# Masked attention: the values' products and the second chunk's turned rows issued behind the first scores, the fifth tile's rows normalised inside the first step

## What is computed

```python
def _L1_xattn_ref(q, k, v, mask, Wq, bq, Wk, bk, Wv, bv, Wo, bo):
    Q = _split_heads(q @ Wq.T + bq)
    K = _split_heads(k @ Wk.T + bk)
    V = _split_heads(v @ Wv.T + bv)
    scores = jnp.einsum('bhqd,bhkd->bhqk', Q, K) / math.sqrt(DV)
    scores = jnp.where(mask, jnp.asarray(1e-09, scores.dtype), scores)
    attn = jax.nn.softmax(scores, axis=-1)
    ctx = jnp.einsum('bhqk,bhkd->bhqd', attn, V)
    ...
    return ctx @ Wo.T + bo
x = x + _L1_xattn_ref(_layernorm(x, axis=-1), ctx_1024, ctx_1024, mask_1x1xSxS2_bk0, ...)
```

## Time and profile before

| what | value |
|---|---|
| median of 3 runs | 1599.02 us (1591.99 to 1600.58) |
| the profiled execution, its own time | 1598.18 us |
| its span, first to last instruction | 1596.4 us |
| what lies around the span | 1.78 us |
| mean granted clock of PE | 0.973 of full speed |
| busy in the span: PE, DVE, ACT, POOL | 1481.8, 1183.3, 881.6, 493.4 us |

### The profile page before, as it was taken

One profiled execution on the slowest core, in us unless ns is written; L12 is line 12 of the kernel. 1 busy time (PEld: TensorE's weight loads), 2 busy tenths in 40 slices (PEclk: granted clock), 3 DMA queues, 4 the chain that ended last, 5 costly groups with the idle time before them and its releaser, 6 DMA issues. The chain is left out here.

```text
span 1596.4 us, 30696 instructions
## 1 busy us (share of the span) xinstructions
PE 1481.8 (93%) x10998; PEld 1088.1 (68%) x11022; DVE 1183.3 (74%) x2306; ACT 881.6 (55%) x2091; POOL 493.4 (31%) x436
## 2 busy tenths in 40 slices
PE   6789999999999999789998997999999977998997
PEld 4567777777777777534443456888888866776785
DVE  4467887786777765368887966888888856788876
ACT  1334443334444344456557836888888874664332
POOL 0122222222222221200001534545555433665333
PEclk9799999999999999989999998999999998999999
DMA  6501111110111101113303810000000006215641
GB/s 243 202 7 50 43 43 53 65 42 8 36 34 34 42 12 76 43 73 145 135 12 122 359 52 2 3 2 3 3 3 4 3 1 263 81 75 169 206 159 58
DMA packets 47280, 118.35 MB, mean 74 GB/s; under 512 B 9406, under 2 KB 15934, under 8 KB 45504
## 3 DMA queue, kind: packets, MB, share of 16 engines
q1 hardware_dynamic: 41488, 100.03, 17.5%
q0 software_dynamic: 5680, 16.85, 2.7%
HBM read 78.89 MB, written 39.80 MB: 74 GB/s over the span
## 5 line engine op out<-in xcount | busy, mean ns | idle before, releaser
L1684 ACT ACTIVATE c_probs<-c_score,c_minus_top 128x128 f32<-128x128 f32 x512 | 183.7, 423 | 1.5 <-DVE c_minus_top L1781 1.5
L1642 POOL TENSOR_TENSOR c_probs<-c_probs,c_recip 128x1024 f32<-128x1024 f32 x64 | 121.5, 1899 | 175.7 <-DVE c_recip L1787 175.7
L629 POOL TENSOR_TENSOR a_attn_lo_parts<-a_attn,a_attn_hi_parts 128x512 fp32r<-128x512 f32 x64 | 80.3, 1288 | 250.0 <-ACT a_attn_hi_parts L695 250.0
L1684 ACT ACTIVATION_READ_ACCUMULATOR c_probs<-c_score,c_minus_top 128x1 f32 x512 | 134.2, 262 | 0.0
L691 ACT COPY a_attn<-a_pv_ps 128x512 f32<-128x512 f32 x64 | 37.0, 578 | 162.6 <-PE a_pv_ps L965 162.6
L928 PE MATMUL a_bank<-a_x_hi_parts,a_wq_hi 128*128 128x256 f32 x512 | 107.8, 293 | 4.3 <-POOL a_x_lo_parts L625 4.3
L928 PE MATMUL a_bank<-a_x_lo_parts,a_wq_hi 128*128 128x256 f32 x512 | 104.3, 286 | 0.0
L655 ACT ACTIVATE a_q<-a_bank,a_shift,a_gain 128x256 f32<-128x256 f32 x64 | 32.3, 556 | 130.2 <-PE a_bank L919 130.2
L928 PE MATMUL a_bank<-a_x_hi_parts,a_wq_lo 128*128 128x256 f32 x512 | 104.1, 285 | 0.0
L2204 ACT CAST d_xT_hi<-d_turn 128x512 fp32r<-128x512 f32 x71 | 41.7, 587 | 110.9 <-PE d_turn L2448 103.9
L911 PE MATMUL a_bank<-a_wo_hi,a_attn_hi_parts 128*128 128x512 f32 x256 | 102.3, 400 | 0.0
(11 more groups left out here) (302 smaller groups left out, 4337.4 us busy)
## 6 DMA issues: line engine op xcount, KB each, us to landing
hidden<-b_hidden SPq DMA_DIRECT2D x5, 2816.0 KB, 8.1
b_hidden<-hidden SPq DMA_DIRECT2D x5, 2816.0 KB, 11.4
xres<-in_x SPq DMA_DIRECT2D x8, 1024.0 KB, 14.1
d_we<-in_we SPq DMA_DIRECT2D x8, 1024.0 KB, 13.0
xres<-in_w_gate_up SPq DMA_DIRECT2D x7, 1024.0 KB, 5.2
d_got<-rows SPq DMA_DIRECT2D x20, 258.0 KB, 2.9
xres<-rows SPq DMA_DIRECT2D x19, 258.0 KB, 2.8
a_rot<-in_rot SPq DMA_DIRECT2D x16, 256.0 KB, 3.1
```

Of the source, the lines that this page charges most:

```text
L629: nc.gpsimd.tensor_tensor(of_spread(attn_lo, g), of_spread(attn, g), of_spread(attn_hi, g), ALU.subtract).then_inc(attn_lo_ready, 1)
L1642: nc.gpsimd.tensor_tensor(part, part, recip[:, t % 2, heads].unsqueeze(2).to_broadcast([P, HALF, KEYS]), ALU.mult).then_inc(scaled, 1)
L1684: last = nc.scalar.activation(probs[:, t, at, :], score_ps[:, h, g, :], ACT.Exp, bias=minus_top[:, h, g:g + 1], accum_out=total[:, t, at:a ...
```

## The change

Three things are put in another place; none is added or removed.

1. On PE the queries of chunk 0 and the scores of tile 0 come directly behind the turned rows of tiles 0 and 1. Behind the scores stand the turned rows of tiles 2 and 3, and behind those the values.
2. On DVE `c_x_lo_parts` of tiles 2 and 3 goes into the first step, behind both `find_tops` of tile 0. The normalising of tile 4 goes behind the first `invert`, with the two additions that write `c_vals` in its middle. `c_wo_lo` goes to the end of the first step.
3. On POOL `deviation` and `add_bias` of tile 4 go behind the first `scale` of tile 0.

The waits follow: PE waits for the values only at the first `weigh`. The diff, cut to its core:

```diff
-        PRE = ["act"] * KB + ["act"] * KB + ["dve"] * NT + ["dve"] * B + ["act"] * KB + ["dve"] * NT
-        PRE_K, PRE_T, PRE_V = KB, 2 * KB, 2 * KB + NT
-        PRE_Q, PRE_T2 = PRE_V + B, PRE_V + B + KB
+        PRE = ["act"] * KB + ["act"] * KB + ["dve"] * NT + ["act"] * KB + ["dve"] * NT + ["dve"] * B
+        PRE_K, PRE_T, PRE_Q = KB, 2 * KB, 2 * KB + NT
+        PRE_T2, PRE_V = PRE_Q + KB, PRE_Q + KB + NT
...
-                deviation(2 * NT, 0)
-                add_bias(2 * NT)
...
                             scale(tile, t, 0)
+                        if isinstance(n, int) and tile == 0:
+                            deviation(2 * NT, 0)
+                            add_bias(2 * NT)
...
-                for b in range(B):
-                    dve.wait_ge(bank_full, PRE_V + b + 1)
-                    nc.vector.tensor_tensor(vals[:, b], bank[(PRE_V + b) % NB][:].rearrange("p (h d) -> p h d", d=DH1),
-                                            bv[:].rearrange("p (h d) -> p h d", d=DH1), ALU.add).then_inc(freed["dve"], 1)
-                dve.wait_ge(weight_hi, 2)
-                nc.vector.tensor_tensor(wo_lo[:], wo[:], wo_hi[:], ALU.subtract).then_inc(weight_lo, 1)
-                for tile in range(NT):
-                    x_low(NT + tile, 1, tile, bank[(PRE_T2 + tile) % NB])
-                norm_stats(2 * NT, 0)
-                norm_row(2 * NT, 0)
-                head = ch.k
+                head, FIRST_STEPS = ch.k, 2
+
+                def beside_first(part):
+
+                    if part == 0:
+                        for tile in range(NT):
+                            x_low(NT + tile, 1, tile, bank[(PRE_T2 + tile) % NB])
+                        return
+                    norm_stats(2 * NT, 0)
+                    for b in range(B):
+                        dve.wait_ge(bank_full, PRE_V + b + 1)
+                        nc.vector.tensor_tensor(vals[:, b], bank[(PRE_V + b) % NB][:].rearrange("p (h d) -> p h d", d=DH1),
+                                                bv[:].rearrange("p (h d) -> p h d", d=DH1), ALU.add).then_inc(freed["dve"], 1)
+                    norm_row(2 * NT, 0)
...
                             find_tops(tile, j, t, 1)
+                        if first:
+                            beside_first(0)
...
                             invert(tile, t, 0)
+                        if first:
+                            beside_first(1)
...
                             x_low(tile + 2 * NT, j, t, use(n, j, t, "T").out)
+                        if first:
+                            dve.wait_ge(weight_hi, 2)
+                            nc.vector.tensor_tensor(wo_lo[:], wo[:], wo_hi[:], ALU.subtract).then_inc(weight_lo, 1)
...
                 for t in range(NT):
                     turn_x(t, t, pre_begin(PRE_T + t))
+                pe.wait_ge(weight_lo, 1)
+                pe.wait_ge(freed["dve"], ring.count("dve", PRE_Q))
+                for m in range(KB):
+                    project(pre_begin(PRE_Q + m), 0, m)
+                pe.wait_ge(freed["act"], PRE.count("act"))
+                scores(0, 0, 0, 0)
+                for t in range(NT):
+                    turn_x(NT + t, t, pre_begin(PRE_T2 + t))
                 pe.wait_ge(ld_wv, 16)
                 for b in range(B):
...
-                pe.wait_ge(weight_lo, 1)
-                pe.wait_ge(freed["dve"], ring.count("dve", PRE_V))
-                for m in range(KB):
-                    project(pre_begin(PRE_Q + m), 0, m)
-                for t in range(NT):
-                    turn_x(NT + t, t, pre_begin(PRE_T2 + t))
-
-                pe.wait_ge(freed["act"], PRE.count("act"))
-                scores(0, 0, 0, 0)
...
-                                pe.wait_ge(freed["dve"], PRE.count("dve"))
+                                pe.wait_ge(freed["dve"], ring.count("dve", PRE_V))
...
+                            if isinstance(tile, int) and tile == 1:
+                                pe.wait_ge(freed["dve"], PRE.count("dve"))
```

More of the change, by code:

```diff
@@ L1818, in _ @@
                     norm_row(tile, tile % 2)
-                for b in range(B):
-                    dve.wait_ge(bank_full, PRE_V + b + 1)
-                    nc.vector.tensor_tensor(vals[:, b], bank[(PRE_V + b) % NB][:].rearrange("p (h d) -> p h d", d=DH1),
-                                            bv[:].rearrange("p (h d) -> p h d", d=DH1), ALU.add).then_inc(freed["dve"], 1)
-                dve.wait_ge(weight_hi, 2)
-                nc.vector.tensor_tensor(wo_lo[:], wo[:], wo_hi[:], ALU.subtract).then_inc(weight_lo, 1)
-                for tile in range(NT):
-                    x_low(NT + tile, 1, tile, bank[(PRE_T2 + tile) % NB])
-                norm_stats(2 * NT, 0)
-                norm_row(2 * NT, 0)
-                head = ch.k
+                head, FIRST_STEPS = ch.k, 2
[10 more added lines that the diff above has]
+                    norm_row(2 * NT, 0)
                 def body(n, j, b, b_before, b_next):
                     if left(n, 2):
-                        ch.base, ch.k = n * DVE_STEPS + head, 0
+                        ch.base, ch.k = n * DVE_STEPS + (head + FIRST_STEPS), 0
+                    if isinstance(n, int) and n == 0:
+                        ch.base = head
                     for t, s in enumerate(plan(n)):
                         tile = n * NT + t
+                        first = isinstance(n, int) and tile == 0
                         if t < NT:
@@ L1856, in body @@
                             x_low(tile + 2 * NT, j, t, use(n, j, t, "T").out)
-                    assert not left(n, 3) or ch.k == DVE_STEPS, ch.k
+                        if first:
+                            dve.wait_ge(weight_hi, 2)
+                            nc.vector.tensor_tensor(wo_lo[:], wo[:], wo_hi[:], ALU.subtract).then_inc(weight_lo, 1)
+                    assert not left(n, 3) or ch.k == DVE_STEPS + (FIRST_STEPS if isinstance(n, int) and n == 0 else 0), ch.k
                 all_chunks(dve, body)
```

## The result

The changed kernel takes 1601.58 us (median of 20 runs, 1598.27 to 1603.38); over the same number of runs the kernel before takes 1595.9 us (1591.99 to 1600.58). The ratio is 1.0031, 95% interval [1.0023, 1.0039]: 4.9 us slower by 1595.9 x 0.0031, between 3.7 and 6.2; the two medians themselves lie 5.7 us apart. The profiled execution of the changed kernel took 1598.27 us, as long as that of before (1598.18). So positions are given from here on as distances from that matmul, **M**. The stage, from M to the first instruction of the expert stage on POOL, took 386.5 us before (1327.71 - 941.21) and 390.3 us now (1327.70 - 937.42).

A forecast was written before the change was run, and what follows sets the result against it. PE was taken to bound the masked stage, with the place that matters its pipeline fill, 6.28 us idle ahead of PT0. Terms 1.95 + 0.5 + 0.1, say 2.6 us, took 1598.18 to 1600.8; range 1594.6 to 1606.1.

The forecast's parts named there:

- third rival: PE's clock falls already in the new gaps of 1.5 and 0.6 us, delaying the exponentials 2.9 us: 1603.7; chance 0.1.
- the fifth: Rival: the start's shift is lost in later stages, the expert stage starting at another clock phase: 1597.9 to 1603.7; chance 0.09.
- forecast 2.45: On PE, PT0 and all behind it come 2.45 us later: idle time ends 1.95 later, plus 0.5 for turning tile 4.
- Step 10: Rest of step one: `c_wo_lo` makes POOL's second scaling end about 2.2 us late, costing PE 0.1 us at PT2.
- second rival: At the second scaling DVE waits for POOL, so tile 1's maxima come 1.2 us past 986.2: 1602.0; chance 0.12.
- due place: The exponentials of tile 1 on ACT were due at 986.2, which is 983.76 + 2.45.
- cover of 0.4 us: Tile 1's maxima stand at 985.8, its exponentials are due at 986.2; without this cover each further DVE microsecond costs one.
- step 9: PE's clock falls in the idle time ahead of PT0 and returns 5.9 us after restart, as before: no extra cost.
- The bound of 2.9 us either way: Bounds on PE's clock cost: no low stretch, or a second of the same length; half of 5.9 us.
- The drain behind a table load: Rival: a drain follows ACT's table load, so the exponentials start 1.4 us later: 1602.2; chance 0.03.

The follow-up runs named there:

- e2: Changed kernel with ACT's query of Qa put behind the exponentials of tile 0, in the first step alone; ratio to before 0.9991.
- b1: Kernel before, with ACT's query of Qa put behind the exponentials of tile 0 in the first step; ratio to before 1.0001.
- f3: Changed kernel with `c_wo_lo` back in the prologue and PE's first idle time filled by computing query block Qb five times; ratio to before 1.0012.
- f1: Kernel before, with PE's idle time ahead of PT0 filled by computing query block Qb five times instead of once; ratio to before 0.9997.
- e1: Changed kernel with `c_wo_lo` made at the end of the prologue again, ahead of the first `find_tops`; ratio to before 1.0023.
- f2: Changed kernel with PE's first idle time filled by computing query block Qb five times instead of once; ratio to before 1.0035.
- g3: Kernel before, with one part of the change alone: `c_wo_lo` made at the end of the first step; ratio to before 0.9999.
- g1: Changed kernel with PE's second idle time, ahead of PT0 of tile 1, filled by computing a query block three times; ratio to before 1.0016.
- g2: Changed kernel with both PE idle times filled, the query block computed five times in tile 0's step, three times in tile 1's; ratio to before 1.0020.

## Why the prediction was right, and where it was short

- **The mechanism held, step by step.** Forecast on the clock of before and found, moved to the same clock by the 3.79 us between the two M: first mask 960.4, found 960.5; query of Qa 969.75, found 969.65; first exponential 971.5, found 971.44; tile 4's rows released by `c_xn` 977.8, found 977.79; PT0 near 978.7, found 978.67. The waits of 1.5 us ahead of the first query matmul and of 0.6 us ahead of the first scores are there (1.61 and 0.56), and the clock did not fall in them, which was the third rival. Nor was the shift lost behind the stage, the fifth: from the first instruction of the expert stage to the end of the span it is 268.7 us before (1596.4 - 1327.71) and 268.8 now (1596.5 - 1327.70). e2 shows what the exponentials waited for, b1 that it is no gain by itself, and the distance of f3 to f1 that this part costs 2.4 us at PT0 of tile 0 and 2.8 at those of tiles 1 and 2 (forecast 2.45).
- **Step 10 failed: the 0.1 us for `c_wo_lo`.** I read from the earlier trace rows that POOL waits for DVE. There the addition and `c_wo_lo` start within 0.02 us of each other (958.95 and 958.96), so the row says nothing of a case in which POOL is well ahead. In the changed kernel the scaling was 0.40 us ahead, and DVE waited. The trace of before had a row that warned of it, 0.07 us behind the start of a POOL addition at 956.29 and 1.48 us long instead of 0.55:

```profile
956.36 1.48 DVE L1764 TENSOR_SCALAR c_xn<-xres,c_mv,c_rstd 128x512 f32<-128x512 f32 x1 [0.67 <-POOL c_rstd L1630]
```

  So the second rival happened in kind: the maxima of tile 1 are late, and its exponentials start 3.06 us behind those of before, where 2.45 was forecast; that is 0.6 past their due place, where the rival had 1.2. e1 gives the price of the collision in the changed kernel, 1.42 us at PT0 of tile 1; f2 against f3 gives 2.9 us with PE at full clock. The rule of the Trainium skill (GPSIMD Engine Reference, 1. Specifications), that GPSIMD shares its SBUF interfaces with VectorE and that they contend when the DVE instruction has two SBUF inputs, agrees with these rows: 3.65 and 3.31 us against 2.28 and 1.27.
- **Where the cover of 0.4 us went.** Where DVE is in time, the exponentials of tile 1 start 1.60 us behind PT2, the turned probabilities of tile 0's second half (before 40.95 and 42.55, g3 41.04 and 42.64, e1 42.59 and 44.18). Where DVE is late, they start 2.57 us behind `find_tops` (changed kernel, 43.04 and 45.61). In g3 `find_tops`, at 39.84, would allow 42.41, and PT2 comes later: the collision is covered by 0.2 us. In the changed kernel PT2, at 42.58, would allow 44.18, and DVE is 1.43 us later: the price that e1 found. Counted from PT0, `find_tops` is only 0.37 us later in the changed kernel than in g3 (5.58 against 5.21), but PT2 is 1.29 us earlier (5.12 against 6.41), because the low clock ended sooner. So most of the cover went with the low clock of step 9, and at most 0.4 us of it with what the change put into the lists of DVE and POOL. Steps 9 and 10 were priced apart and are not independent: what the clock gave back, DVE took.
- **Step 9, the clock, was right in sum and wrong in its parts.** The first low stretch lasted 4.1 us from PE's restart and not 5.9, which gives 1.2 us back (the distance to before falls from 2.8 at PT0 to 1.63 at the next turned probabilities); a second fall, which I did not forecast, costs 1.1 (g1). The bound of 2.9 us either way covers both.
- **The sum in the profile,** at PT0 of tile 2: 2.82 (PT0 of tile 0) - 1.19 (clock) + 1.41 (`c_wo_lo`) + 1.08 (second fall) = 4.12 us, forecast 2.6. The measured 4.9, interval 3.7 to 6.2, holds the one and not the other. The range held, and so did the call that the change moves the time by less than 0.5%; 20 runs told 0.3% from nothing, which is finer than the 0.5% that I had allowed. The range was set by the scatter of three runs, 8.6 us, so that it held says little about the mechanism. That the measured 1601.58 lies so near the 1600.8 given is luck: I started from 1598.18, and the median of before over 20 runs is 2.3 us lower, while the change cost 2.3 us more than forecast.
- **The drain behind a table load**, which the Trainium skill (ScalarE: Activation LUTs, What ACT_TABLE_LOAD costs) states, is not there in this trace: the load ends at 967.63 and the exponential starts at 967.65.

## What to carry to other kernels

Moving work behind a milestone gains nothing if the engine that consumes the milestone has something older in its list that waits for the moved work: read the lists of all engines that follow, the untouched ones above all. Here one query on ACT, not touched by the change, turned 7.6 us of earlier maxima into 0.8 us of later exponentials, and exchanging it with the exponentials turned a loss of 0.3% into 0.1% less than before (not clear of nothing), and into a clear gain of 0.4% with `c_wo_lo` put where DVE idles. When an operation of DVE and one of POOL meet, as `c_wo_lo` and the scaling do here, find out from rows which of them begins first and by how much, and price both cases. And when one term of a sum lets an engine come sooner, ask again what the others had as cover: here 1.2 us that PE won from its clock uncovered DVE.

## What the hardware did that was not expected

- `c_wo_lo`, a DVE operation with two SBUF inputs, and an operation of POOL did not run beside each other. With POOL ahead by 0.25 (e1) to 0.78 us (g3), POOL kept its time (the scaling its 1.90; in e1 it was an addition of 1.47 us, itself begun behind `c_xn`), `c_wo_lo` took 3.26 to 3.65 us instead of 2.28, and the POOL addition behind it 3.31 to 3.33 instead of 1.27. With the two recorded starts 0.01 to 0.02 us apart, POOL's the earlier (before, b1, f1), it was the addition that took 3.44 us, and `c_wo_lo` kept 2.28; which of the two really came first there, the record cannot tell. The 1.48 us of `c_xn` show the same wait for a DVE operation with one SBUF tensor.
- A wait of the same length does or doesn't make PE's clock fall: it fell around PT0 of tile 1 behind waits of 1.81 us (e1) and 1.87 us (g2), not behind 1.89 (before) or 1.83 (f3). What decides between them stays open.
- Open as well: f1's 2.7 us, in its profile and not in its time, and e2's 3.2 against before, of which the time shows 1.4.
